# Vision tower on one core: embedding weights centred on the chip, the tokens' means summed elsewhere, x loaded in three parts

## The reference, cut to what matters

```python
embedded = einsum('bnk,kd->bnd', patches, Wp) + bp          # k = 768 = 6 x 128, d = 64
pos      = relu(xy @ W1 + b1) @ W2 + b2
h = embedded + pos
h = h + attn0(layernorm(h))      # layernorm: (x - mean) / sqrt(var + 1e-5) over the 64 channels
h = h + ffn0(layernorm(h))
h = h + attn1(layernorm(h))
h = h + moe(layernorm(h))
```

## Time and profile before

| | us |
|---|---|
| median of the three runs | 74.75 (74.56 to 74.87) |
| the profiled execution | 74.51 |
| its span, first to last instruction | 72.7 |
| TensorE busy (share of span) | 64.6 (89%) |
| VectorE busy | 41.9 (58%) |
| ScalarE busy | 29.2 (40%) |
| GpSimd busy | 13.0 (18%) |
| dummies on TensorE (L687, 63 records) | 19.9 |
| mean granted clock of TensorE, of full speed | 0.992 |
| read from HBM | 3.82 MB |

### The profile page before, as it was taken

The page is one execution under the profiler, slowest core; times in us unless marked ns, Lnnn a source line. Parts: engine busy times, 40 slices in busy tenths (PEclk is TensorE's granted clock), DMA queues, the critical chain, the costliest instruction groups (busy, mean ns, idle before and its releaser), DMA issues.

```text
span 72.7 us, 1994 instructions
## 1 busy us (share of the span) xinstructions
PE 64.6 (89%) x843; PEld 39.5 (54%) x843; DVE 41.9 (58%) x108; ACT 29.2 (40%) x63; POOL 13.0 (18%) x29
## 2 busy tenths in 40 slices
PE   3995996999999999989979969799999889999930
PEld 1330554777887585445435645577954285543910
DVE  2590199484799983536642397997540157429430
ACT  0330104404497821296925060488023748530030
POOL 6800094000004920538030000000000030000000
PEclk9999999999999999999999999999999999999996
DMA  0799999900000000000000000000000000000003
GB/s 5 180 394 390 373 224 263 265 16 0 0 9 0 0 9 0 0 0 5 0 0 0 0 0 9 0 9 0 0 9 5 0 0 0 0 0 0 0 0 72
DMA packets 2389, 4.07 MB, mean 56 GB/s; under 512 B 779, under 2 KB 1229, under 8 KB 2381
## 3 DMA queue, kind: packets, MB, share of 16 engines
q1 hardware_dynamic: 1840, 3.55, 16.8%
q10 hardware_dynamic: 509, 0.40, 1.7%
q0 software_dynamic: 32, 0.00, 0.1%
HBM read 3.82 MB, written 0.13 MB: 54 GB/s over the span
## 4 chain that ended last, share of the span: by engine, by line
PE 64%; DVE 13%; DMA 9%; ACT 4%; POOL 3%; issue 3%; DVEq 0%; ACTq 0%; POOLq 0%
PE psum L687 10%; DMA Xt<-in_x_dram 9%; PE psum L681 6%; DVE top L503 3%; POOL WoS L298 3%; PE psum L697 3%; PE psum L893 3%; PE psum L939 3%; PE psum L789 3%; PE psum L740 3%; PE psum L991 3%; PE psum L1032 2%; PE psum L716 2%; DVE E L601 2%; DVE top L599 2%
## 5 line engine op out<-in xcount | busy, mean ns | idle before, releaser
L687 PE MATMUL psum<-warm 128*128 128x512 bf16 x63 | 19.9, 429 | 1.2 <-DVE warm L455 1.2
L687 PEld LDWEIGHTS psum<-warm 128*128 128x128 bf16 x63 | 5.8, 107 | 8.1 <-issue 4.3
L298 POOL TENSOR_TENSOR WoS<-pack_attn,top 128x256 f32<-128x256 f32 x5 | 3.1, 647 | 11.1 <-DVE top L510 11.1
L468 DVE TENSOR_TENSOR onehot<-idb,iota 128x2048 bf16<-128x2048 bf16 x4 | 4.8, 1244 | 0.0
L326 POOL TENSOR_TENSOR resT<-hT,xC 128x256 f32<-128x256 f32 x1 | 0.7, 724 | 20.5 <-DVE xC L630 20.5
L405 ACT ACTIVATE E<-E 128x512 f32<-128x512 f32 x4 | 2.5, 630 | 3.2 <-DVE E L601 3.1
L348 ACT ACTIVATE lv<-psum,eps 128x256 f32<-128x256 f32 x4 | 1.9, 473 | 3.5 <-PE psum L729 0.9
L599 DVE TENSOR_REDUCE top<-psum 128x8 f32<-128x512 f32 x4 | 2.7, 686 | 0.4 <-PE psum L908 0.4
L434 ACT ACTIVATE ge<-psum,pack_moe 128x512 f32<-128x512 f32 x4 | 2.5, 679 | 1.1 <-PE psum L991 1.1
L908 PE MATMUL psum<-kT,qT 9*64 9x64 f32 x128 | 2.1, 231 | 0.9 <-DVE qT L587 0.7
L773 PE MATMUL psum<-top,pack_ident 128*128 128x256 f32 x12 | 2.9, 387 | 0.0
(11 more groups left out here) (200 smaller groups left out, 131.7 us busy)
## 6 DMA issues: line engine op xcount, KB each, us to landing
Xt<-in_x_dram SPq DMA_DIRECT2D x1, 1024.0 KB, 6.4
Xt<-in_x_dram SPq DMA_DIRECT2D x1, 512.0 KB, 7.5
pack_both<-in_both_dram SPq DMA_DIRECT2D x2, 240.2 KB, 8.8
pack_moe<-in_moe_dram SPq DMA_DIRECT2D x1, 450.0 KB, 9.8
pack_mid<-in_mid_dram SPq DMA_DIRECT2D x1, 327.5 KB, 10.0
pack_attn<-in_attn_dram SPq DMA_DIRECT2D x1, 288.0 KB, 8.1
pack_expert<-in_expert_dram SPq DMA_DIRECT2D x2, 130.0 KB, 9.3
pack_wp<-in_wp_dram ACTq DMA_DIRECT2D x1, 192.0 KB, 6.0
```

The source lines that it names most:

```text
L298: gp.tensor_tensor(WoS[:, s, 4 * u:4 * u + 4, :].rearrange("p (b n) d -> p b n d", b=2), bc(WoT[:, 2 * u:2 * u + 2, :], 1, 2), bc(top0[:, ...
L468: ve.tensor_tensor(onehot[:, 16 * k:16 * k + 16, :], bc(idb[:, k, :], 1, 16), iota16[:, :, :], ALU.is_equal).then_inc(s_hot, 1)
L687: mm(B[bank][:, :], lhsT=warm[:, 0:P], rhs=warm[:, :], start=True, stop=True)
```

## The change

* `wp` is issued by SP, ahead of x, and no longer by ScalarE; x comes in three transfers of two k blocks each.
* VectorE sums each row of the embedding weights (and of `posW2`) over the 64 channels and takes the mean away: `Wpc`, `posc`. The embedding with them lands centred in `B[1]`; the copy to `hT0`, the wait for it and the centring matmul L721 fall out of the way to the square. `hT0` is copied behind the square and is now centred.
* `last_rows(0)` is put between k blocks 3 and 4, the head products are split around the variance matmul, two of the first 12 dummies and the four around `last_rows` go. `centre` and the last three `hot` change order on VectorE.
* The mean that the tokens lack is rebuilt in `B[3]` by matmuls with the weight means (`token_mean`), in places where dummies stood; ScalarE copies it to `meanT` before the queries of attn1, and GpSimd adds it to `hT2` (`hM`) for the final residual. Banks of `last`, of the gate weights and of the ffn hidden tiles move so that `B[3]` is free.
* Slot 0's sum and reciprocal are made in two halves of four heads. Of the `WoS` halves GpSimd now makes (0,0), (0,1), (1,0), (1,1), (2,0), (3,1), ScalarE (2,1), behind the copy of slot 0's mix, and VectorE (3,0).

```diff
-            load(Xt[:, :, 0:4, :], packs["x"][:, :, 0:4, :], in_x[0])
-            load(Xt[:, :, 4:6, :], packs["x"][:, :, 4:6, :], in_x[1])
+            load(pack["wp"][:, :], packs["wp"], in_wp)
+            for i in range(3):
+                load(Xt[:, :, 2 * i:2 * i + 2, :], packs["x"][:, :, 2 * i:2 * i + 2, :], in_x[i])
             load(pack["attn0"][:, :], packs["attn0"], in_attn0)
...
-            def scaled_Wo(s):
-
-                pool.wait_ge(s_rinv, s + 1)
-                for u in ((0, 1), (0,), (0,), (1,))[s]:
...
+            pool.wait_ge(s_wsum, 3)
+            gp.tensor_scalar(wmean[:, 0:KX], wsum[:, 0:KX], 1.0 / D, None, ALU.mult).then_inc(s_wmean, 1)
+            gp.tensor_scalar(wmean[0:D + 2, KX:KX + 1], wsum[0:D + 2, KX:KX + 1], 1.0 / D, None, ALU.mult).then_inc(s_wmean, 1)
+
+            def scaled_Wo(s, u, ready):
+
+                pool.wait_ge(s_rinv, ready)
...
+            scaled_Wo(0, 0, 1)
+            scaled_Wo(0, 1, 2)
+            scaled_Wo(1, 0, 3)
+            scaled_Wo(1, 1, 3)
+            scaled_Wo(2, 0, 4)
+            scaled_Wo(3, 1, 5)
...
+            pool.wait_ge(s_hm_ev, 1)
+            pool.wait_ge(s_h2, 1)
+            gp.tensor_tensor(hM[:, :], hT[2][:, :], meanT[:, :], ALU.add).then_inc(s_h2, 1)
             pool.wait_ge(s_x, 4)
-            pool.wait_ge(s_h2, 1)
-            gp.tensor_tensor(resT3[:, :], hT[2][:, :], xC[3][:, :], ALU.add).then_inc(s_res3, 1)
+            pool.wait_ge(s_h2, 2)
+            gp.tensor_tensor(resT3[:, :], hM[:, :], xC[3][:, :], ALU.add).then_inc(s_res3, 1)
...
             act.dma_start(ids[:, :], I["L1_attn_edge_index"][1, :].rearrange("(p e) -> p e", p=P)).then_inc(in_ids, 16)
-            act.dma_start(pack["wp"][:, :], packs["wp"]).then_inc(in_wp, 16)
             act.dma_start(pack["pos"][0:D + 2, :], packs["pos"][0:D + 2, :]).then_inc(in_pos, 16)
             act.dma_start(pack["ident"][:, :], packs["ident"]).then_inc(in_ident, 16)
...
+                if k == 0:
+                    sc.activation(hT[0][:, :], HC[:, 0:HALF], ACT.Copy).then_inc(s_h, 1)
...
-            act.wait_ge(s_emb, 1)
-            sc.activation(hT[0][:, :], B[0][:, 0:HALF], ACT.Copy).then_inc(s_h, 1)
             deviation(0)
...
             act.wait_ge(s_shift, 1)
-            for i in range(HEADS):
-                ins = sc.activation(E0[:, 0, i, :], B[i // 4][:, i % 4 * TOK:(i % 4 + 1) * TOK], ACT.Exp,
-                                    bias=shift[:, i:i + 1], scale=SC0)
-            ins.then_inc(s_exp0, 1)
+            for u in range(2):
+                for i in range(4 * u, 4 * u + 4):
+                    ins = sc.activation(E0[:, 0, i, :], B[i // 4][:, i % 4 * TOK:(i % 4 + 1) * TOK], ACT.Exp,
+                                        bias=shift[:, i:i + 1], scale=SC0)
+                ins.then_inc(s_exp0h, 1)
...
-            act.wait_ge(s_rinv, 2)
+            mixed(0)
+            act.wait_ge(s_rinv, 4)
             for i in range(4, HEADS):
-                ins = sc.activation(WoS[:, 1, i, :], WoT[:, 2 + i % 2, :], ACT.Copy, scale=top0[:, 2, 1, i:i + 1])
+                ins = sc.activation(WoS[:, 2, i, :], WoT[:, 2 + i % 2, :], ACT.Copy, scale=top0[:, 2, 2, i:i + 1])
             ins.then_inc(s_wosa, 1)
-            mixed(0)
...
-                sc.activation(hid[:, k, :].rearrange("p (c t) -> p c t", c=2), psum[:, 2 * k:2 * k + 2, 0:HALF],
+                sc.activation(hid[:, k, :].rearrange("p (c t) -> p c t", c=2), psum[:, 4 * k:4 * k + 2, 0:HALF],
...
+            act.wait_ge(s_hm, 1)
+            sc.activation(meanT[:, :], B[3][:, 0:HALF], ACT.Copy).then_inc(s_hm_ev, 1)
...
+            def centred(dst, src, sums, n):
+                ve.tensor_reduce(sums, src, X, ALU.add).then_inc(s_wsum, 1)
+                dve.wait_ge(s_wsum, n)
+                ve.scalar_tensor_tensor(dst, bc(sums, len(src.shape) - 1, D), -1.0 / D, src, ALU.mult, ALU.add).then_inc(s_wpc, 1)
+
+            dve.wait_ge(in_wp, 16)
+            centred(Wpc[:, 0:2, :], Wp[:, 0:2, :], wsum[:, 0:2], 1)
+            centred(Wpc[:, 2:KX, :], Wp[:, 2:KX, :], wsum[:, 2:KX], 2)
             hot(0)
+            dve.wait_ge(in_pos, 16)
+            centred(posc[:, :].unsqueeze(1), posW2.unsqueeze(1), wsum[0:D + 2, KX:KX + 1], 3)
+            hot(1)
+            hot(2)
+            hot(3)
             dve.wait_ge(in_ident, 16)
             dve.wait_ge(s_blk, 3)
             ve.tensor_tensor(centre[:, :], ident, mean64[:, :], ALU.subtract).then_inc(s_centre, 1)
-            hot(1)
-            hot(2)
-            hot(3)
...
+            def softmax0_sum(s, heads, done):
+                ve.tensor_reduce(top0[:, 1, s, heads], E0[:, s, heads, :], X, ALU.add).then_inc(s_sum0, 1)
+                dve.wait_ge(s_sum0, done)
+                ve.reciprocal(top0[:, 2, s, heads], top0[:, 1, s, heads]).then_inc(s_rinv, 1)
...
-            softmax0_sum(0)
+            for u in range(2):
+                dve.wait_ge(s_exp0h, u + 1)
+                softmax0_sum(0, slice(4 * u, 4 * u + 4), u + 1)
             for s in range(1, SLOTS):
-                softmax0_sum(s)
-            for s, u in ((2, 1), (3, 0)):
-                dve.wait_ge(s_rinv, s + 1)
+                dve.wait_ge(s_exp0, s)
+                softmax0_sum(s, slice(0, HEADS), s + 2)
+            for s, u in ((3, 0),):
+                dve.wait_ge(s_rinv, 5)
...
             pe.wait_ge(s_warm, 1)
-            keep_clock(1, WARM)
-
-            pe.wait_ge(in_wp, 16)
-            pe.wait_ge(in_x[0], 16)
-            for q in range(4):
+            keep_clock(1, WARM - 2)
+
+            def embed(q):
                 for c in range(2):
-                    mm(B[0][rows[c], 0:HALF], lhsT=Wp[:, q, :], rhs=Xt[:, c, q, :], start=(q == 0), stop=False)
-                if q == 1:
-                    pe.wait_ge(in_pos, 16)
...
-            pe.wait_ge(s_warm, 2)
-            for c in range(2):
-                mm(B[0][rows[c], 0:HALF], lhsT=posW2, rhs=bc(posh[:, :], 1, 2), start=False, stop=False)
-            pe.wait_ge(in_x[1], 16)
-            for q in range(4, KX):
-                for c in range(2):
-                    ins = mm(B[0][rows[c], 0:HALF], lhsT=Wp[:, q, :], rhs=Xt[:, c, q, :], start=False, stop=(q == KX - 1))
-            ins.then_inc(s_emb, 1)
+                    ins = mm(B[1][rows[c], 0:HALF], lhsT=Wpc[:, q, :], rhs=Xt[:, c, q, :], start=(q == 0), stop=(q == KX - 1))
+                return ins
...
-            pe.wait_ge(s_centre, 1)
-            pe.wait_ge(s_h, 1)
-            mm(B[1][:, 0:HALF], lhsT=centre[:, :], rhs=hT[0][:, :], start=True, stop=True).then_inc(s_hc, 1)
-            pe.wait_ge(in_attn0, 16)
-            for k in range(4):
+            def head_products(k):
+
                 for c in range(2):
                     mm(B[6][rows[c], k * D:(k + 1) * D], lhsT=Wq0[0:D, k, :], rhs=Wk0[0:D, :], start=True, stop=True)
                     ins = mm(B[5][rows[c], k * D:(k + 1) * D], lhsT=Wq0[D:P, k, :], rhs=Wk0[D:P, :], start=True, stop=True)
-            ins.then_inc(s_g, 1)
+                return ins
+
+            def token_mean(q):
+
+                pe.wait_ge(s_wmean, 1)
+                for c in range(2):
+                    ins = mm(B[3][rows[c], 0:HALF], lhsT=wmean[:, q:q + 1].broadcast_to([P, D]), rhs=Xt[:, c, q, :],
+                             start=False, stop=(q == KX - 1), skip_group_check=True)
+                return ins
+
+            pe.wait_ge(s_wpc, 1)
+            pe.wait_ge(in_x[0], 16)
+            embed(0)
+            embed(1)
+            pe.wait_ge(in_pos, 16)
+            mm(B[4][0:D, 0:P], lhsT=posW1, rhs=grid, start=True, stop=True).then_inc(s_posh, 1)
+            pe.wait_ge(s_wpc, 2)
+            pe.wait_ge(in_x[1], 16)
+            embed(2)
+            embed(3)
+            last_rows(0)
+            pe.wait_ge(s_wpc, 3)
+            pe.wait_ge(s_posh_ev, 1)
+            pe.wait_ge(s_warm, 2)
+            for c in range(2):
+                mm(B[1][rows[c], 0:HALF], lhsT=posc[:, :], rhs=bc(posh[:, :], 1, 2), start=False, stop=False)
+            pe.wait_ge(in_x[2], 16)
+            embed(4)
+            embed(5).then_inc(s_hc, 1)
+            pe.wait_ge(in_attn0, 16)
+            head_products(0)
+            head_products(1)
             pe.wait_ge(s_sq, 1)
             mm(B[2][:, 0:HALF], lhsT=mean64[:, :], rhs=sq[0][:, :], start=True, stop=True).then_inc(s_var, 1)
-            keep_clock(3, 2)
-            for k in range(4):
+            head_products(2)
+            head_products(3).then_inc(s_g, 1)
+            for k in range(1, 4):
                 last_rows(k)
-            keep_clock(3, 2)
             pe.wait_ge(s_x, 1)
             pe.wait_ge(s_g_ev, 2)
...
+                pe.wait_ge(s_wos, (2, 4, 5, 6)[s])
+                if s == 2:
                     pe.wait_ge(s_wosa, 1)
-                elif s >= 2:
-                    pe.wait_ge(s_wosd, s - 1)
+                elif s == 3:
+                    pe.wait_ge(s_wosd, 1)
...
+            pe.wait_ge(s_exp0h, 2)
```

(31 more changed lines are left out.)

## The result

Four executions of the changed kernel took 74.15, 74.11, 72.69 and 72.75 us (median 73.43); the kernel before took 74.66 on the same chip (74.56 to 74.87). The ratio is 0.974 with an interval of 0.970 to 0.978: **1.97 us faster**, where 2.8 were forecast. It leaves out executions more than 1.5% above the fastest of their kernel, so it goes by the two short ones; median against median the gain is 1.23. The profiled execution is the one of 74.15 (span 72.4), a long one; no short execution of this kernel was profiled.

A forecast was written before the change was run, and what follows sets the result against it. Bound: a chain of waits through x's arrival, then TensorE or what hands it operands. Gain 2.9 - 0.05 - 0.06 = 2.8; 72.0 us predicted, own range 71.5 to 72.6, 8-of-10 range 71.4 to 73.2.

The forecast's parts named there:

- the head: Kernel start up to the queries: they start at 13.0 instead of 15.96, taken as 2.9 us won.
- (a): Rival: `ident` stays late, so `last_rows(0)` waits for `row_pow`: 72.7, or 72.9 with `pos` late; chance 0.18.
- (b): Rival: transfers pay for their number, 0.40 each; x whole at 9.7, `attn0` at 11.0, time 72.7; chance 0.08.
- (c): Rival: GpSimd bounds the WoS stage, 0.4 lost there and 0.43 at one `token_mean`: 72.8; chance 0.07.
- WoS stage: Scaling of `WoS` up to mix 1: 0.06 lost, bounds 0.1 won to 0.4 lost.
- Arrival of x: Loads at the start: x's three parts land at 5.95, 7.47 and 8.87, `attn0` still at 10.2.
- VectorE: Three sums and three centrings add 1.95, paid by 3.4 us idle; weights ready at 4.85 and 5.8.
- Embedding: TensorE's k blocks, `last_rows(0)` and position term: centred bank complete at 10.25 instead of 12.24, 2.0 earlier.
- Head products: Eight ahead of the variance matmul, behind `attn0` at 10.2: run 10.25 to 10.6, fit with no slack left.
- xS and exponent shift: VectorE's new work beside the queries: 0.05 lost, from nothing to 0.3.
- The rest: Token means in dummies' places: nothing, within 0.1 either way; `meanT` copy and GpSimd's addition in waits or idle time.
- (d): Rival: TensorE's clock falls to 1.2 GHz in pauses before x's second and third part and stays: 75.8; chance 0.04.

The follow-up runs named there:

- e1: Changed kernel with the variance matmul ahead of the wait for `attn0` and all head products behind it: median 72.78 us (profiled 72.59), ratio 0.972.
- e6: Kernel before with only the loads changed (`wp` first on SP's queue, x in three parts): median 74.63 us, ratio 0.994.
- e4: Changed kernel with `wp` issued first on ScalarE's queue, ahead of `ids`: 77.42 us, ratio 1.025.
- e7: e4 with the wait for `attn0` and the head products behind the variance matmul and 11 dummies at the start: 80.17 us, ratio 1.059.
- e11: e4 with 15 dummy matmuls at the start instead of 10: 73.31 to 80.80 us, median 78.40.
- e3: Changed kernel with x in two transfers (1 MB and 512 KB): median 78.32 us, no ratio.
- e9: Changed kernel with each pair of token-mean products replaced by a pair of dummy matmuls: 73.99 us, ratio 0.978.
- e0: Changed kernel run again without an edit: median 74.1 us, ratio 0.973.
- e2: Changed kernel with `attn0` issued ahead of x's third part: median 74.86 us, no ratio.
- e8: Changed kernel with the variance matmul ahead of the wait for `attn0` and the head products, and 13 dummies at the start: median 73.86 us, ratio 0.974.
- e10: e8 with the sharing of the weights' scaling (WoS) as before, slot 0's sums whole again: 72.53 to 73.94 us and one of 78.16, ratio 0.977.
- e5: Changed kernel with 13 dummy matmuls at the start instead of 10: median 72.98 us, ratio 0.971.

## Why the prediction was right or wrong

**Direction and mechanism right, one term too large.** By the ratio the time is in the range (0.974 of 74.66 is 72.7, and 71.4 to 73.2 was said); the plain median of the four, 73.43, is above it. The step that failed is the head: 2.9 was forecast, 1.43 is in this trace and 1.78 in the best one (e1). The forecast's own sign of being wrong, queries after 13.7, came in every trace (14.09 at the earliest). That 72.7 still lies in the range is owed to its upper end, which was drawn to take in rivals (a) to (c), none of which is shown to have happened, and to 0.2 won in the WoS stage where a loss was forecast.

**Arrival of x.** The forecast for 5.95, 7.47 and 8.87 held the excess of 400 kB and the old rates. Measured 6.7, 7.9, 9.8: at 9.8 some 2530 kB had moved where 2380 were reckoned, and they moved more slowly. e6 has the same landings with nothing else changed, so it is the new loading that makes x late, not the rest of the change. Of its two edits it is `wp` ahead of x, not the number of parts: with `wp` on the other queue and three parts x was whole at 8.5 to 9.3 (e4, e7, e11), with `wp` ahead of it at 9.7 to 11.4 in all ten traces of that kind, e3 with its two parts among them (11.1). `wp` first takes bytes from x's start, and `attn0` came to 11.2 to 12.8 in all traces with this order, never 10.2.

**VectorE.** The count of 1.95 for six operations was right (1.41 for the weights, 0.43 for `posc`: 1.84), the start wrong by 0.9 (5.11 against 4.25), since `wp` beside `ids` delays it. The Trainium skill, "DMA: Bandwidth & Descriptors", section Queues, rings and completion order, says that an engine of the DMA goes in turns between its queues; that agrees with 1.8 against 2.9 us. It cost nothing here: the first blocks need only the part ready at 5.7, and the second is there before block 2.

**Embedding.** Blocks start 0.70 late and the work is 0.25 longer than said (from start to start `last_rows(0)` 0.48 against 0.40 and position term 0.48 against 0.43, last blocks 1.03 against 0.89); the last is a misreading of the earlier trace rows, whose 0.89 counts from the end of the position term: in the timeline the last blocks took 1.03 before as well. The centred bank came at 11.2 instead of 10.25. Even in the best trace TensorE has no pause left there: with these instructions it is the embedding's own length, behind x's first part, that sets the bank.

**Head products.** "They fit, with no slack left" did not hold: in the profiled execution TensorE waited 0.5 us for `attn0`, which landed at 11.7 and not 10.2. The edit that takes the wait away (e1) is not shown to win it back, since the head products then stand behind the variance. Together: 0.95 + 0.5 = 1.45 of the 1.53 by which the queries missed 13.0.

**xS and exponent shift.** 0.05 lost was forecast; Q to M is 3.20 or 3.21 wherever the queries ran at the full rate, and 3.20 before: nothing lost.

**WoS stage.** 0.06 lost was forecast, 0.29 won up to mix 1 measured. From there to LN1 it took 0.09 more than before (3.84 against 3.75), also with dummies in the token means' places (e9), so they aren't the cause; it was not searched further. In all 0.2 won. The bound "0.1 won" was too tight: the exponentials' early half was left out, and with it slot 1's reciprocal came 0.12 later behind the first maximum (4.34 in e1, 4.22 before), not 0.30, so that GpSimd's six half tiles ran 0.62 apart without a wait.

**The rest.** Token means at nothing, within 0.1: 0.05 (e9). The stretch behind LN1: 43.7 in most traces, 44.1 in this one.

**Sum over e1**: 1.78 - 0.01 + 0.20 - 0.05 (43.76 against 43.71) = 1.92, measured 74.51 - 72.59 = 1.92.

**The profiled execution's 74.15** is 1.56 above e1's 72.59: 0.35 at the queries, and a further 1.2: the hole of 0.62 in the scores (with what hangs on it 0.85) and one of 0.64 at 45.56 behind [L to end 44.1]. Of the other traces e0 has one of 0.76 at 45.8 and none in the first scores, the kernel before one of 0.27 at 46.6. TensorE waits there for nothing that the profile shows. The Trainium skill, "Runtime: NRT & Kernel Launch", section Instruction fetch mechanics, calls the cost of the sequencer's next page mostly hidden; if these are such fetches, they are not hidden here. No run tested that: the cause stays open.

**Rivals.** (a) is false: `ident` lands at 6.2 and `last_rows(0)` waits for nothing. (b) named 9.7 for x, 11.0 for `attn0` and 72.7, and nearly these numbers came (9.8, 11.7; 72.7 from the ratio). That is luck: its mechanism, a price of 0.40 for each transfer that SP issues more, would put x at 8.9 + 0.4 = 9.3 in e4, e7, e11 and e3 alike, and it came at 9.3, 8.6, 8.5 and 11.1. The fixed 2.0 us that the prediction took from the Trainium skill, "DMA: Bandwidth & Descriptors", section Anatomy of one DMA, are stated there for transfers issued by GpSimd, not by SP; the 10.9 for x worked out from them lies within what was measured with `wp` ahead (9.7 to 11.4), but no run shows a fixed price behind it. (c) is false: GpSimd's stage gained. (d) was rated too low. The lower level appeared in the head of e2, e3, e4, e7, e8, e9 and e10 at 1.1 us and more, and the kernel before has it too: on the last chip five of its 13 executions took 76.4 to 78.0, at a mean granted clock of 0.977. So it belongs to both kernels and doesn't turn the comparison, and none of the four executions of the result was longer than 74.15, so (d)'s 75.8 didn't come; but it spreads the executions by more than any single edit here moves them. Whether the changed kernel falls to the lower level more often than the one before is not shown. That no edit of the changed kernel (e1, e5, e8) beats it is all that the intervals allow.

## What to carry to other kernels

A small transfer put ahead of a large one is paid for by everything behind it and by what shares the engines on the other queue: look at both before moving a load forward, and price the last part's landing, not the first's. A wait for data stands in TensorE's queue ahead of all that follows, so look at which matmul the chain needs and which one's operand is late; that swapping them pays was not shown here (e1), because the work put behind comes back a little later. Where the head of a kernel is short, look at the duration of one known matmul in each profiled execution before comparing two traces: 1.08 or 1.98 for the same eight records is worth more than most edits.

## What the runs showed of the hardware

- **Half the rate at a recorded clock of 1.00.** In e9 the windows from 5.5 to 13.0 us all show PEclk 1.00, while eight records of 256 columns take 1.98 instead of 1.08; the same in e2, e4 and e7. Only e3, e8 and e10 have 0.50 in the record of the head, and there the same eight records take the same 1.98 (e3) and 1.97 (e10), from which the lower level is inferred where the record says 1.00. The first dummies of the changed kernel are such a case: ten took 4.45 us at a recorded 1.00, and six later ones 1.40. The Trainium skill, "TensorE: Matmul & The Clock Gate", section Seeing it yourself, warns that the gate's trace events have been unreliable; the traces agree.
- **The level is not a function of the program.** Same instructions and nearly the same pause (changed and e9), different level; and the six executions of e11 have mean clocks from 0.93 to 1.00. The Trainium skill, the same page, section What's actually happening, says that the gate's monitor runs free of the kernel's start; that agrees, but no run here tests it.
- **The lower level is kept through dense work.** In e3 TensorE was busy for 9.97 of the 10.0 us from 8.5 to 18.5 and stayed at 0.50; in e8 it fell to 0.50 between 14 and 15 us, with no pause above 0.48 from 6.67 on.
- **Landings of one program differ by 1.5 us**: x's last part at 9.8 and 11.3, `attn0` at 11.7 and 12.8, at equal issue times.
- **A transfer slows one on the other queue**: the same 64 KB of `ids`, issued at 0.72, took 1.8 us with x first on SP's queue and 2.9 to 3.1 with `wp` first there; behind `wp` on its own queue they took 4.2 to 4.4 from their issue.
